# Attention one: each key block's products of probabilities and values issued as two query ranges, at two places of the order

## The reference, cut to what matters

```python
xh = x.reshape(b, c, h, he).transpose(0, 2, 1, 3)
qkv = jnp.einsum('bhce,ef->bhcf', xh, Wqkv) + bqkv
q, k, v = jnp.split(qkv, 3, axis=-1)
att = jnp.einsum('bhqe,bhke->bhqk', q, k) / jnp.sqrt(jnp.float32(he))
mask = jnp.tril(jnp.ones((c, c), dtype=att.dtype), k=-1)
att = jax.nn.softmax(att * mask, axis=-1)
out = jnp.einsum('bhqk,bhke->bhqe', att, v)
out = out.transpose(0, 2, 1, 3).reshape(b, c, d)
out = out @ Wr + br
```

## Time and profile before

| | |
|---|---|
| median of 3 runs | 3106.49 us (3102.18 to 3107.34) |
| span of the profiled execution | 3102.6 us |
| PE busy | 2739.3 us, 88% |
| DVE busy | 2505.2 us, 81% |
| POOL busy | 1897.6 us, 61% |
| ACT busy | 1468.1 us, 47% |
| scores on PE (L604) | 518.2 us, 1536 matmuls |
| products on PE (L618) | 329.3 us, 3072 matmuls |

### The profile page before, as it was taken

The page is one execution under the profiler, slowest core; times in us unless marked ns, Lnnn a source line. Parts: engine busy times, 40 slices in busy tenths (PEclk is TensorE's granted clock), DMA queues, the critical chain, the costliest instruction groups (busy, mean ns, idle before and its releaser), DMA issues. The chain is left out here.

```text
span 3102.6 us, 64827 instructions
## 1 busy us (share of the span) xinstructions
PE 2739.3 (88%) x14614; PEld 1558.5 (50%) x14614; DVE 2505.2 (81%) x9025; ACT 1468.1 (47%) x3554; POOL 1897.6 (61%) x3733
## 2 busy tenths in 40 slices
PE   3788898898889888889868999999999799999998
PEld 1344344444344444344345666666666466666666
DVE  4577777787777787777556999999999799999998
ACT  1455555565556565556513555555555322222222
POOL 3773444444444444444344777777777588888887
PEclk7788898898898898899868999999999899999999
DMA  2433223223323223323130000000000000000000
GB/s 39 86 73 42 32 30 42 28 34 41 38 24 41 34 28 41 42 25 38 22 132 1 1 1 0 0 0 0 0 0 0 1 9 14 14 14 14 14 15 17
DMA packets 60208, 79.78 MB, mean 26 GB/s; under 512 B 20364, under 2 KB 32408, under 8 KB 59416
## 3 DMA queue, kind: packets, MB, share of 16 engines
q1 hardware_dynamic: 55240, 67.74, 15.5%
q0 software_dynamic: 3072, 8.39, 0.9%
q10 hardware_dynamic: 1744, 2.16, 0.2%
HBM read 18.98 MB, written 8.39 MB: 9 GB/s over the span
## 5 line engine op out<-in xcount | busy, mean ns | idle before, releaser
L455 ACT ACTIVATE probs<-scoresT 128x512 f32<-128x512 f32 (+3 forms) x1536 | 692.7, 491 | 526.8 <-PE scoresT L604 518.6
L546 DVE TENSOR_REDUCE cand<-ring 128x4 f32<-128x512 f32 (+3 forms) x1280 | 592.1, 518 | 83.7 <-PE ring L653 79.8
L376 POOL TENSOR_SCALAR_AFFINE_SELECT probs<-probs 128x128 f32<-128x128 f32 x1024 | 292.6, 295 | 537.9 <-ACT probs L455 532.5
L604 PE MATMUL scoresT<-stage 98*128 98x512 bf16 (+3 forms) x1536 | 518.2, 379 | 68.2 <-ACT probs L455 62.1
L653 PE MATMUL ring<-stage 96*128 96x128 bf16 (+3 forms) x2304 | 403.5, 280 | 42.0 <-DMA stage<-parts 14.3
L653 PEld LDWEIGHTS ring<-stage 96*128 96x128 bf16 x2304 | 175.9, 98 | 328.4 <-DVE cand L546 122.7
L618 PE MATMUL pv<-probs,Vg 128*32 128x512 f32 (+3 forms) x3072 | 329.3, 535 | 4.4 <-POOL probs L376 4.3
L604 PEld LDWEIGHTS scoresT<-stage 98*128 98x128 bf16 x1536 | 146.4, 101 | 274.3 <-ACT probs L455 219.3
L553 DVE CUSTOM_DVE_ANT_0 ring<-ring,lower 128x128 f32<-128x128 f32 x1024 | 260.6, 319 | 18.5 <-PE ring L653 18.5
L1125 ACT ACTIVATE hT<-mmT,w_be,w_g 128x128 f32<-128x128 f32 x512 | 185.4, 468 | 155.4 <-PE mmT L1055 155.4
L1064 PE MATMUL mm<-w_W,x2T 128*128 128x512 f32 x512 | 257.6, 626 | 0.0
(11 more groups left out here) (254 smaller groups left out, 5657.7 us busy)
## 6 DMA issues: line engine op xcount, KB each, us to landing
stage<-parts SPq DMA_DIRECT2D x256, 96.0 KB, 3.1
stage<-parts SPq DMA_DIRECT2D x256, 64.0 KB, 3.3
stage<-parts SPq DMA_DIRECT2D x256, 32.0 KB, 3.0
out<-result SPq DMA_DIRECT2D x64, 128.0 KB, 1.7
stage<-ct SPq DMA_DIRECT2D x128, 4.0 KB
w_W<-in_W SPq DMA_DIRECT2D x4, 512.0 KB
h<-in_WT,tok POOLq DMA_INDIRECT x64
stage<-in_tok_ SPq DMA_DIRECT2D x1, 1024.0 KB, 6.4
```

The lines of the kernel that those rows point to most:

```text
L376: nc.gpsimd.affine_select(out=d, in_=d, compare_op=ALU.is_gt, fill=0.0, base=0, pattern=[[1, P]], channel_multiplier=-1).then_inc(mask_ok, 1)
L455: nc.scalar.activation(probs[:, n % 8, lo:hi], scoresT[u % SCORE_BANKS][:, lo % 512:(hi - 1) % 512 + 1], ACT.Exp, scale=SOFT).then_inc(exp ...
L546: ins = nc.vector.tensor_reduce(c[:, i, j:j + n], src[:, P * at:P * (at + n)].rearrange("p (a b) -> p a b", a=n), AX.X, ALU.max)
L604: nc.tensor.matmul(scoresT[u % SCORE_BANKS][:, lo % 512:(hi - 1) % 512 + 1], Ks[0:ROWS, gi, hh, P * kt:P * kt + P], Qs[0:ROWS, gi, hh, lo: ...
```

## The change

The event `PV` gets a third field. "late" covers the queries from 512 on (for `kt` from 4 on, the block's whole range), "early" those up to 512 (only `kt` under 4). The late part of block `kt`-1 stands after the second head's score of block `kt`, the early part after the fourth head's. `pv_ok` is counted once for each block, by the early part for `kt` under 4 and by the late part after that. The late part of blocks 0 to 3 does not wait for the mask.

```diff
@@ -94,7 +94,7 @@
     if tail:
-        at(pos_of["PV_COPY"], ("PV", -1, 7), ("PV_COPY", -1))
+        at(pos_of["PV_COPY"], ("PV", -1, 7, "late"), ("PV_COPY", -1))
@@ -131,8 +131,10 @@
             events.append(("S", kt, h))
-            if h == HPG - 1 and kt >= 1:
-                events.append(("PV", 0, kt - 1))
+            if h == 1 and kt >= 1:
+                events.append(("PV", 0, kt - 1, "late"))
+            if h == HPG - 1 and 1 <= kt <= TPB // 2:
+                events.append(("PV", 0, kt - 1, "early"))
@@ -605,19 +607,22 @@
                         elif kind == "PV":
-                            rel, kt = e[2:]
+                            rel, kt, part = e[2:]
                             v = G + rel
                             par = (gi + rel) % 2
-                            if kt == 0:
+                            if kt == 0 and part == "late":
                                 wait(pe, pvS_ok, 2 * v)
                                 pe.wait_ge(vg_ok, v + 1)
-                            pe.wait_ge(mask_ok, 32 * v + 4 * kt + 4)
+                            if part == "early" or kt >= 4:
+                                pe.wait_ge(mask_ok, 32 * v + 4 * kt + 4)
                             pe.wait_ge(exp_ok, UNITS * v + score_units(kt, HPG - 1)[-1][0] + 1)
-                            for lo, hi in ((P * kt, 512), (512, S)) if kt < 4 else ((P * kt, S),):
-                                for hh in range(HPG):
-                                    ins = nc.tensor.matmul(pv[32 * hh:32 * hh + 32, lo:hi], Vg[:, par, kt, hh, :],
-                                                           probs[:, (4 * kt + hh) % 8, lo:hi], start=(kt == 0),
-                                                           stop=(kt == (3 if hi == 512 else 7)), tile_position=(0, 32 * hh))
+                            lo, hi = (P * kt, 512) if part == "early" else (max(P * kt, 512), S)
+                            for hh in range(HPG):
+                                ins = nc.tensor.matmul(pv[32 * hh:32 * hh + 32, lo:hi], Vg[:, par, kt, hh, :],
+                                                       probs[:, (4 * kt + hh) % 8, lo:hi], start=(kt == 0),
+                                                       stop=(kt == (3 if hi == 512 else 7)), tile_position=(0, 32 * hh))
+                            if part == "late" and kt < 4:
+                                continue
                             ins.then_inc(pv_ok, 1)
```

## The result

The changed kernel takes 3153.91 us (median of 4 runs, 3152.62 to 3154.33) against 3105.26 for the kernel before on the same chip (one run more than in the table above): 1.0158 of its time, 95% interval 1.0143 to 1.0172, so 48.7 us slower. The forecast had the direction and 28.5 us; the time lies outside the range (3096 to 3148).

What follows compares the result with a forecast made beforehand. It took PE, then DVE's maxima, to bound window 0 and DVE nearly window 1; 0.7 + 0.5 + 0.45 + 0.4 - 0.15 = 1.9 us a pair, times 15, made 3106.5 + 28.5 = 3135 us, range 3096 to 3148.

Steps and rivals of the forecast that it cites:

- The direction: The whole kernel would get slower; forecast, wait-bound and free-cut cases together were given 0.69.
- Step (2): Price on PE of splitting a burst: 0.13 us to leave and 0.09 to enter, 0.23 a cut.
- (3): Window 0, PE's own stretch: three cuts, blocks 0 to 2, add 0.7 us.
- Rival D: A cut is free but late banks stay: 0.8 us for a pair, 3118 us; chance 0.06.
- Step (4): Window 0: block 4's earlier burst and block 3's cut make DVE wait at bank 8 of head 2, +0.5 us.
- Step (5): Window 0: block 5's earlier burst waits for POOL's mask, delaying bank 5 of head 3, +0.45 us.
- Step (6): Window 1: cuts are outweighed by filled waits for ACT, but bank 5 of head 2 comes late, +0.4 us.
- Step (7): Windows' ends: block 6's earlier burst fills PE's 0.26 us wait for ACT, -0.15 us at one end.
- The sum: Local terms added to 1.9 us for each pair of windows; 15 pairs give 28.5 us.
- a moved clock as a sign against me: A clock digit of the first half that moves would show the forecast wrong; no size given.
- A: Starved ACT counts: window 1's waits and DVE gaps vanish, -1.9 us a pair there; faster, 3094 us; chance 0.17.
- C: POOL's mask wait is the bound: 1 us in each window, +1.55 a pair on top, 3158 us; chance 0.06.

Runs made afterwards that it cites:

- full_cuts: full_before plus only the cuts of blocks 0, 1 and 2 in window 0: 3068.77 us, ratio 0.9875 to the kernel before.
- full_before: Kernel before plus extra matmuls while PE waits for cf and after the scores at positions 1 to 4 of window 0: 3074.22 us, ratio 0.9895.
- moves_only: Kernel before with the bursts of blocks 4, 5 and 6 moved up in both windows, no cuts: 3134.61 us, ratio 1.0104.
- full_after: Whole change plus the fillers of full_before, with 14 and 13 matmuls before cf: 3102.52 us, ratio 0.9985 to the kernel before.
- w1_only: The change in window 1 alone, window 0 as in the kernel before: 3106.41 us, ratio 1.0001.
- dose2: Kernel before plus 2 extra matmuls of 512 columns behind block 1's products in window 0: 3099.99 us, ratio 0.9982.
- only5: Kernel before with only block 5's burst in window 0 moved from position 27 to 25: 3103.66 us, ratio 0.9991.
- filled: Whole change plus five extra matmuls before PE's wait for the mask in window 0: 3152.23 us, ratio 1.0151 to the kernel before.
- pool_first: Whole change, with POOL in window 0 running head 2's MAX_FINAL after the mask of block 5's fourth head: 3135.03 us, ratio 1.0098 to the kernel before.
- cf_filled: Kernel before plus 12 and 11 extra matmuls while PE waits for cf in windows 0 and 1: 3068.78 us, ratio 0.9879.
- best_w0: best without its part in window 1 (no cuts of blocks 1 and 2, block 6 at its old place): 3066.93 us, ratio 0.9882 to the kernel before.
- best: Kernel before plus fillers, block 0 cut in window 0, blocks 1 and 2 cut and block 6 moved in window 1: 3055.48 us, ratio 0.9840.
- block5_again: Repeat run of the whole change with block 5's burst in window 0 back at position 27: 3152.90 us, ratio 1.0152 to the kernel before.

## Why the prediction was wrong in size

**The direction** came from the right view: PE busy for 24.79 of 25.00 us just where the cuts stand.

**Step (2) and (3), the cut.** Right as a local cost: 0.76 us for three in the changed kernel against 0.7, and a burst of 512 columns there still takes 1.00 to the next start (899.81 to 900.81). Rival D falls for the kernel as it is. With the clock held, the same three cuts gain 0.16 us a window (full_cuts), where block 0's late burst fills a wait for xn that PE does not have in the kernel before (the XT group takes 1.53 us there, 2.13 in full_before). The Trainium skill's sentence that a change of the tiling mode drains the engine ("TensorEngine Tiling (Array Packing)", Key Properties) agrees with these steps; that the drain of a matmul hides behind the next one ("TensorE: Matmul & The Clock Gate", Step-by-step: what each phase is for) is not seen at this change of mode.

**Step (4).** Right: 0.62 and 0.65 against 0.5.

**Step (5).** The wait, its place and its cause (POOL behind DVE's maximum) were right, and the gap was 0.48 against 0.45 in those windows of moves_only and full_after where the clock stayed up over the burst. In the changed kernel the clock was at 1.2 GHz behind it, the burst took 1.44 us instead of 0.78, and the term was 1.50. This is the largest term that was mis-sized; yet putting block 5 back did not return it.

**Step (6).** A gap of 0.62 for 0.4 is in the trace, but w1_only shows no cost. I counted one late bank and did not see that DVE's other gaps would shrink as much: in place of the 1.35 and 0.57 us stand five that sum to 1.86.

**Step (7).** No gain at the ends is seen.

**The sum is the step that failed.** It took each local delay to reach the end of the pair one for one, with PE's clock as it was ("each microsecond that PE adds before that bank moves the window's end", "while PE remains the bound"). I had listed a moved clock as a sign against me, but gave it no term, though 0.95 stood beside the very stretch that I read the earlier trace rows. The clock falls to 1.2 GHz around each wait for cf, and the groups behind it (WR, PT, XT) run at half speed until it rises. The runs show that the place of that rise is not tied to the work: WR took 2.21, 2.26, 2.65, 2.98 and 3.62 us in dose2, only5, before, after and filled, for the same eight matmuls. So a delay of 0.4 us ahead of it can cost nothing, and a saving can be lost. In the changed kernel 3.40 us come out of terms that were forecast at 1.9; where the clock is held over a whole pair of full_after, 0.92 us do. That makes 14 us over 15 pairs (an estimate from these pairs, with a few fillers more in the one kernel than in the other), so most of the 49 us goes with the clock. With most of the low clock filled away, the difference is 28 us, the same number as my sum by other terms: the cuts and block 0 gain there, and 15 us are the clock's falls behind the wait for the mask. That match is chance.

**The rivals.** A was no story of this kernel. PE's waits of 0.36 and 0.41 us for ACT did go in window 1, as A and the forecast said, but the window became no shorter (w1_only). With the clock held, the two cuts and block 6's place earn 0.5 us of A's 1.9 there; the whole change in window 1 earns nothing even then (39.46 against 39.39). C named the wait for POOL as the bound: the wait is there in 15 windows 0 and in no window 1 of the loop, and pool_first got 19 us back by removing it. It comes nearest in time (3158) without its mechanism, which wanted a wait in both windows.

**Open:** by which rule the clock falls and rises, so why block 5 put back gives 0 and POOL's order 19, and why 12 windows 0 of moves_only lose the clock behind the wait and 2 do not; and the 6 us that dose2 gains. What is shown is that the time follows the clock's falls and rises, and that keeping PE busy over the waits holds the clock and gives 33 to 37 us (full_before, cf_filled, best_w0), 50 with the parts of best. That the whole excess of 20 us over the forecast is the clock's was not isolated: no run held it fully in the changed kernel, only single pairs of full_after.

## What to carry to other kernels

A periodic kernel whose PE clock falls in every period does not add up delays: look at the clock in each stretch of one period before pricing anything, and try to fill the waits first. After that, moves of a few tenths of a microsecond can be measured for what they are. A burst moved up in PE's order takes along its waits: look at what the releasing engine has in its own queue before the release.

## What was not expected of the hardware

- Extra matmuls whose result is thrown away made the kernel 1.2% faster (3068.78 for 3105.67), as PE's clock stayed at 1.00 in window 1 instead of 0.92.
- Within one kernel, full_after, the same wait of 1.35 us was followed by a clock of 2.4 GHz in 3 windows 0 and of 1.2 GHz in 11; and in block5_again the clock fell behind a wait of 0.62 us.
- 0.43 us more work in each window 0 left the pair at 92.16 us (dose2), and three different kernels (changed, block 5 back, filled) had pairs of 95.57 or 95.58.
